# A Mamba and mixture-of-experts kernel: VectorE's products with C get places of their own in the order, their wait on the scan is written first, and the orders of all engines are laid out anew

## The reference, cut to what matters

```python
# first half: a selective scan (Mamba) over ctx, gated by silu(layernorm(x))
x = einsum(in_proj_w, ctx); u = silu(conv4(x) + conv_b)
dt_lo, Bm, Cm = split(einsum(x_proj_w, u))
delta = softplus(einsum(dt_proj_w, dt_lo) + dt_proj_b)
def step(state, xs):                       # 512 channels x 16 states, 512 steps, 4 batches
    dA = exp(d_t[..., None] * A)
    state = state * dA + (d_t * u_t)[..., None] * B_t[:, None, :]
    y_t = einsum('ben,bn->be', state, C_t) # the product with C
    return state, y_t
x2 = x + tanh(g_xattn) * (y + D * u) * silu(z)
# second half: mixture of 8 experts, the best 2 of each token, plus a shared one, on layernorm(x2)
h = gelu(x2n @ wd[e]) * combine[:, e];  out = x2 + tanh(g_ffn) * (sum_e h @ wu[e] + shared)
```

## Time and profile before

| | us |
|---|---|
| median of 3 runs (lowest to highest) | 658.73 (657.96 to 660.96) |
| the profiled execution, its own time | 659.18 |
| span of its trace | 657.4 |
| busy: TensorE, VectorE, GpSimd, ScalarE | 507.8, 507.1, 494.3, 398.7 |

### The profile page before, as it was taken

One profiled execution on the slowest core, in us unless ns is written; L12 is line 12 of the kernel. 1 busy time (PEld: TensorE's weight loads), 2 busy tenths in 40 slices (PEclk: granted clock), 3 DMA queues, 4 the chain that ended last, 5 costly groups with the idle time before them and its releaser, 6 DMA issues.

```text
span 657.4 us, 7506 instructions
## 1 busy us (share of the span) xinstructions
PE 507.8 (77%) x2304; PEld 254.5 (39%) x2304; DVE 507.1 (77%) x560; ACT 398.7 (61%) x757; POOL 494.3 (75%) x240
## 2 busy tenths in 40 slices
PE   5505535688897788954499799975997997989998
PEld 4202211246462355611143233331443443656766
DVE  4577898767999899986877999967879779873211
ACT  4549667788635776494478654454798855671340
POOL 4289999879998859897939989979677799950000
PEclk9657777869797897966599889966999799899989
DMA  2596723543265231346521323054310644001001
GB/s 81 166 388 200 244 64 129 195 176 114 80 210 174 80 117 35 99 165 240 164 90 59 128 86 108 24 193 156 125 61 22 225 160 134 11 1 59 22 17 48
DMA packets 39940, 79.70 MB, mean 121 GB/s; under 512 B 5977, under 2 KB 12761, under 8 KB 39900
## 3 DMA queue, kind: packets, MB, share of 16 engines
q1 hardware_dynamic: 39900, 79.23, 35.7%
HBM read 62.17 MB, written 17.04 MB: 120 GB/s over the span
## 4 chain that ended last, share of the span: by engine, by line
PE 30%; DVE 28%; issue 15%; ACT 13%; POOL 10%; DMA 3%; ACTq 0%; POOLq 0%; DVEq 0%; SPq 0%
DVE decay L1220 10%; PE wk L1528 7%; PE wk L1514 7%; POOL ring L979 7%; DVE ring L1220 6%; PE y_ps L1449 4%; ACT decay L1055 3%; PE wk L1465 3%; DVE ring L1234 3%; DVE u L1246 2%; ACT L1024 2%; DMA dd<-dd_scratch 2%; ACT z L1090 2%; POOL ring L1001 2%; PE wk L1490 1%
## 5 line engine op out<-in xcount | busy, mean ns | idle before, releaser
L979 POOL TENSOR_TENSOR ring<-dd,b_in 128x2048 f32<-128x2048 f32 x64 | 289.2, 4531 | 12.2 <-issue 8.9
L1055 ACT ACTIVATE decay<-dd,a_neg 128x255 f32<-128x255 f32 (+1 forms) x384 | 188.1, 533 | 40.6 <-DVE ring L1220 40.4
L1001 POOL TENSOR_TENSOR ring<-ring,c_in 128x2048 f32<-128x2048 f32 x32 | 144.8, 4525 | 21.9 <-DVE ring L1220 20.7
L1220 DVE TENSOR_TENSOR_SCAN ring<-decay,ring 128x1024 f32<-128x1024 f32 x64 | 144.6, 2278 | 13.6 <-ACT decay L1055 7.0
L1220 DVE TENSOR_TENSOR_SCAN decay<-decay,ring 128x1024 f32<-128x1024 f32 x64 | 146.2, 2285 | 11.2 <-ACT decay L1055 7.8
L1514 PE MATMUL wk<-xc,w_down 128*128 128x256 f32 (+1 forms) x432 | 133.3, 463 | 6.4 <-DVE xc L1302 3.8
L1528 PE MATMUL wk<-h,w_up 128*128 128x256 f32 (+1 forms) x432 | 136.0, 471 | 0.5 <-DVE h L1395 0.5
L1449 PE MATMUL y_ps<-ring,fold 128*32 128x256 f32 (+1 forms) x768 | 79.4, 560 | 60.7 <-DVE ring L1234 60.4
L1514 PEld LDWEIGHTS wk<-xc,w_down 128*128 128x128 f32 x432 | 81.1, 193 | 55.6 <-issue 44.5
L1528 PEld LDWEIGHTS wk<-h,w_up 128*128 128x128 f32 x432 | 83.5, 198 | 44.3 <-issue 35.2
L1234 DVE TENSOR_TENSOR ring<-decay,c_in 128x1024 f32<-128x1024 f32 x64 | 78.4, 1225 | 7.0 <-DVE decay L1220 0.5
(11 more groups left out here) (105 smaller groups left out, 444.3 us busy)
## 6 DMA issues: line engine op xcount, KB each, us to landing
dd<-dd_scratch SPq DMA_DIRECT2D x64, 256.0 KB, 3.1
dd<-dd_scratch SPq DMA_DIRECT2D x32, 512.0 KB, 4.2
b_in<-bc_scratch SPq DMA_DIRECT2D x8, 512.0 KB, 5.6
...
```

Of the source, the lines that this page charges most:

```text
L979: nc.gpsimd.tensor_tensor(two, dd[:, j % DD_RING:j % DD_RING + 2, None, n:2 * n].broadcast_to([P, 2, TILES[v], n]), b_in[:, None, g % BC_R ...
L1001: nc.gpsimd.tensor_tensor(two, two, c_in[:, None, g % BC_RING].broadcast_to([P, 2, WIDE]), ALU.mult).then_inc(weighed_pool, 2)
L1055: last = nc.scalar.activation(decay[:, i % 2, q * n + 1:(q + 1) * n], dd[:, j % DD_RING, 1:n], ACT.Exp, scale=a_neg[:, c, r, k:k + 1])
L1220: last = nc.vector.tensor_tensor_scan(to, decay[:, i % 2], ring[:, i % RING], 0.0, ALU.mult, ALU.add)
```

## The change

Three things are changed. VectorE's products with C become jobs of `PLAN` ("weigh_d") and leave the loop. In `weigh`, the wait for `scanned` is written ahead of the one for `c_loaded`. The figures of `PLAN` are new for all kinds of jobs on all engines. No instruction that computes is added or removed, and no size changes.

```diff
 POOL_WEIGHS = (0, 1)
+DVE_WEIGHS = tuple(r for r in range(NR4) if r not in POOL_WEIGHS)
...
 PLAN = {
     "y": [
-        [-2.73, 7.3, 9.05, 14.01],
-        [19.76, 23.76, 28.09, 34.17],
+        [-2.78, 7, 8.06, 14.03],
+        [19.9, 23.2, 28.46, 32.48],
...
+    "weigh_d": [
+        [3.5, 4.333, 7.667, 8.333, 11.5, 12.5, 15.667, 16.5],
...
-DVE_DUE = by_slot("conv", "stats_z", "mean read", "scale_x", "lg read", "shares", "mix read", "up read", "gate", "biases")
+DVE_DUE = by_slot("conv", "stats_z", "mean read", "scale_x", "lg read", "shares", "mix read", "up read", "gate", "biases", "weigh_d")
...
             def weigh(i):
                 g = bc_no(PLACES[i][0], PLACES[i][2])
+                dve.wait_ge(scanned, i + 1)
                 dve.wait_ge(c_loaded[g % BC_RING], DMA * (g // BC_RING + 1))
-                dve.wait_ge(scanned, i + 1)
                 nc.vector.tensor_tensor(ring[:, i % RING], decay[:, i % 2], c_in[:, g % BC_RING],
                                         ALU.mult).then_inc(weighed_dve, 1)
...
                     if name == "biases":
                         split_biases()
+                    if name == "weigh_d":
+                        weigh(START[v] + NR4 * (k // len(DVE_WEIGHS)) + DVE_WEIGHS[k % len(DVE_WEIGHS)])
 
             for slot in range(START[NU]):
                 what_is_due(slot)
                 scan(slot)
-                if not weighs_on_pool(slot):
-                    weigh(slot)
             what_is_due(START[NU])
```

More of the change, by code:

```diff
@@ L173 @@
+        [5.28, 5.51, 6.83, 6.92],
+        [23.06, 24.08, 24.43, 25.39],
+        [57.5, 57.71, 58.06, 61.03],
+        [95.02, 95.04, 95.06, 95.18],
+        [107.9, 107.95, 108.09, 111.23],
     ],
     "mean_p": [
[L175 to L180 removed]
+        [17.81],
+        [38.38],
+        [63.76],
+        [95.46],
+        [116.21],
+        [129.85],
     ],
     "mean": [
[L183 to L185 removed]
@@ L186 @@
-        [95.64],
-        [119.49],
-        [130.05],
+        [20.57],
+        [39.29],
+        [64.77],
+        [95.61],
+        [119.25],
+        [130.2],
     ],
     "var_p": [
-        [20.6],
-        [39.24],
-        [65.91],
-        [95.96],
-        [120.45],
-        [131.44],
+        [22.05],
+        [40.14],
+        [66.24],
+        [95.88],
+        [119.83],
+        [131.54],
     ],
     "var": [
-        [21.62],
-        [39.68],
-        [66.21],
-        [96.14],
@@ L203 @@
-        [120.91],
-        [132.83],
+        [22.98],
+        [40.64],
+        [66.47],
+        [95.96],
+        [120.2],
+        [132.87],
     ],
     "lg_t": [
-        [23.59],
-        [41.83],
-        [66.73],
-        [98.03],
-        [122.56],
-        [134.21],
+        [24.8],
+        [42.85],
+        [67.07],
+        [97.71],
+        [122.48],
+        [134.19],
     ],
     "lg": [
-        [24.5],
-        [42.35],
-        [67.39],
-        [99.21],
-        [123.45],
```

414 lines of the change are left out of this document (203 added, 211 removed), and 69 rows, old and new, of the table PLAN.

## The result

The changed kernel takes 643.73 us (median of 4 runs, 643.21 to 644.75) against 658.70 before: ratio 0.9772, 95% interval 0.975 to 0.9793. Its profiled execution took 644.75 us over a span of 643.0.

What follows compares the result with a forecast made beforehand. No engine was taken to own the chain; VectorE and GpSimd run in step through the scan. Terms -2.9 + 2.2 - 1.3 - 1.2 - 0.2 = -3.4 us gave 655.3 us, range 648.5 to 662.5.

Steps and rivals of the forecast that it cites:

- The wait: VectorE's products with C: carrying the wait on `scanned` themselves shortens VectorE's order by 6.7 us, of which 2.9 us was taken.
- the 28 entries: The product's separate wait stands 28 times in the chain of waits; 28 of 64 times 6.7 gave 2.9 us.
- Jobs between scan and product: On VectorE, 14 products get other work ahead of them; these delays of ScalarE's exponentials were costed at nothing.
- The gates: VectorE's gates wait for TensorE's sums; of 24 compared, three were priced: +2.2, -1.3 and -1.2 us.
- gate (1,1): TensorE's sum now precedes dt chunks, so the 3.57 us wait goes; logits' read at 143.35 or up to 1 us after; -1.3 us.
- Gate (4,3): Three scans now cover its 2.33 us wait, but a scan's wait for GpSimd may take it back; half taken, -1.2 us.
- gate (0,1): No scan stands between product 7 and the gate now; its wait grows from 1.33 to 3.5 us, +2.2 us.
- The end: TensorE's `up` (4,3) moves ahead of several `down` chunks and no longer fills the last gelu's wait; -0.2 us.
- The other moves I cost at nothing: DMAs and GpSimd's products move by a slot or two beside GpSimd's 4.5 us instructions; 0 us.
- VectorE sets the pace: Rival, chance 0.26: throughout, all 6.7 us arrive and gates (1,1) and (4,3) give 3.6 and 2.3; 648.1 us.

Runs made afterwards that it cites:

- e1_wait: The kernel before with only the product's two waits swapped, the wait for `scanned` first, all orders as before: 656.20 us, ratio 0.9953.
- e2_order: The changed kernel with the product's two waits back in the old order, all else as changed: 645.27 us, ratio 0.9778.
- e3_adjacent: The changed kernel with each of the 64 products directly behind its scan again: 645.96 us, ratio 0.9793.
- g01: The changed kernel with the figure of gate (0,1) set back, so scan 8 stands between product 7 and the gate again: 644.68 us, ratio 0.9775.
- x_silu: The changed kernel with ScalarE's batch of silus put back behind the logits' copy and the first read of `down`: 655.91 us, ratio 0.9932.
- s_route: e1_wait with unit 2's routing moved and the silu batch ahead of the logits' copy, GpSimd's centring of z not moved: 668.60 us, ratio 1.0140.
- min_silu: e1_wait with the silu batch ahead of the logits' copy and the moves its inputs need, the routing as before: 659.94 us, ratio 0.9999.
- u2_silu: e1_wait with new figures for unit 2's second half, the silu batch ahead of the logits' copy and its inputs moved: 663.31 us, ratio 1.0046.

## Why the prediction was wrong, point by point

**The wait** (-2.9 us) was right in its gap: the products' idle time is 1.7 us against the 1.5 forecast. In the old order it was worth 3.1 us (e1_wait), where the same count gave 2.2. The rule of the Trainium skill, VectorE: DVE Perf Modes, "The DRAIN you can't avoid", that a semaphore costs nothing extra, doesn't hold for a wait that stands as an instruction of its own: e1_wait removes no instruction that computes and its ratio excludes 1. But that the sum came near is luck: the 28 entries ran over the whole scan, and the gain came in slots 84 to 104. Nor does it add to the other terms: e2_order shows 0.4 us of it inside the new order, give or take 2.7, and the changed kernel has no gain in slots 84 to 104 (95.4 us, 95.0 before).

**Jobs between scan and product** (0) was right: e3_adjacent, and 15.8 us of waiting for ScalarE. (Product 119 has three jobs ahead of it, not one or two.)

**The gates** (+2.2, -1.3, -1.2): the three waits were right and none of the prices can be kept. g01 shows that the first costs nothing, and the logits' copy behind gate (1,1) stands 2.9 us later than before in place of up to 1. Together the two give 0.6 us of slots 0 to 24, and the other kernels with the new order there take 99.0 to 101.4 us, those with the old order 98.2 to 99.7, so nothing of the 1.3 shows. Gate (4,3) was priced too low: half was taken since the scan at 533.01 waited for GpSimd, and this wait went too. Slots 111 to 116 are 4.0 us shorter, and they take 21.4 to 22.3 us in the eight kernels with the new order there and 25.7 to 26.4 in the twelve others. How much of it is the gate's isn't shown, as no run took it alone, and 1.7 us of it had been lost in slots 104 to 111. What failed at gate (0,1) is the step that a wait of VectorE is paid in full where it stands: here later waits took it up.

**The end** (-0.2) is open: 0.3 to 1.5 us at a like clock, and the clock of this stretch, which the forecast passed over, moved it by more.

**"The other moves I cost at nothing"** is the step that made the forecast wrong. The sentence named DMAs and products of GpSimd, and passed over ScalarE's batch of silus, 6.8 us in one piece, which moved ahead of the copy of the logits. x_silu prices it at 10.6 us. The comparison went by gates, where VectorE waits for TensorE. What mattered was the row [3.80 <-PE wk L1514] of ScalarE in the trace of before, idle time directly ahead of a long piece of work that needed nothing of it, with VectorE and GpSimd waiting behind. The row alone wouldn't have done: in that trace GpSimd finished z_ln, the batch's input, at 329.74 us, behind `lg_t` at 327.63, and s_route and min_silu show what it costs to move the batch while its input is late. The rival "VectorE sets the pace" (648.1) was nearest in size and wrong in its reason: VectorE still idles 67.2 us of 536.

Of the 14.4 us of span, slots 64 to 84 are 6.5, and the place of the batch is a condition for them, not the cause alone (min_silu, u2_silu). Slots 0 to 64 are 3.5, of which 2.9 lie in slots 24 to 64. Slots 84 to 127 are 3.2. That is the size of what e1_wait has there, but it isn't the wait: e2_order takes 185.7 us with the old waits, and the gain lies in slots 111 to 116 instead of 84 to 104. The 1.5 behind slot 127 goes with the clock and the end's order together. The single moves ahead of slot 64 and behind slot 84 weren't taken apart.
